# Attention stacks held in fixed halves of the rows, and a re-ordered opening, in a fused attention and convolution kernel

## The reference

```python
x = x + _L0_conv_ref(_gn(x), ...)   # 8-head attention over the 1024 pixels, head size 16
x = x + _L1_conv_ref(_gn(x), ...)   # 7x7 depthwise conv, layer norm over channels, MLP of 512, erf gelu
...
q = proj(Wq, bq, xh); k = proj(Wk, bk, xh); v = proj(Wv, bv, xh)
attn = jnp.einsum('bgdi,bgdj->bgij', q, k) * SCALE
attn = jax.nn.softmax(attn, axis=-1)
out = jnp.einsum('bgij,bgdj->bgdi', attn, v)
```

## Time and profile before

| | us |
|---|---|
| Median of 3 runs | 298.36 (298.24 to 299.01) |
| Profiled execution, its own time | 298.37 |
| Span of the profiled execution | 296.4 |
| PE busy | 287.5 (97%) |
| DVE busy | 233.8 (79%) |
| ACT busy | 181.1 (61%) |
| POOL busy | 79.4 (27%) |

### The profile page before, as it was taken

How to read it: one execution, slowest core, us unless ns; L and a number is a source line. 1 busy time by engine, 2 the same in 40 slices (tenths; PEclk the granted TensorE clock), 3 DMA queues, 4 the chain that set the end, 5 groups by cost and what they waited for, 6 DMA issues and landing times.

```text
span 296.4 us, 5468 instructions
## 1 busy us (share of the span) xinstructions
PE 287.5 (97%) x2104; PEld 116.9 (39%) x2106; DVE 233.8 (79%) x264; ACT 181.1 (61%) x354; POOL 79.4 (27%) x103
## 2 busy tenths in 40 slices
PE   7999999999999999999999999999999999999895
PEld 3544443343343443444343343344333444323342
DVE  2749889989989989988869989989995367986331
ACT  2342278878878878878878968875246644011421
POOL 7100633332000000000009788997020200101010
PEclk9999999999999999999999999999999999999999
DMA  7266003203303203303122387300000016720001
GB/s 241 50 121 102 11 0 58 50 8 54 54 3 56 51 9 56 54 3 54 18 40 48 110 169 170 81 1 3 1 2 0 2 26 156 186 83 0 0 35 35
DMA packets 8488, 16.30 MB, mean 55 GB/s; under 512 B 2564, under 2 KB 3716, under 8 KB 8464
## 3 DMA queue, kind: packets, MB, share of 16 engines
q1 hardware_dynamic: 8048, 15.29, 24.1%
q10 hardware_dynamic: 416, 0.69, 1.0%
HBM read 4.96 MB, written 1.73 MB: 23 GB/s over the span
## 4 chain that ended last, share of the span: by engine, by line
PE 90%; DVE 7%; POOL 1%; issue 1%; ACT 0%; DVEq 0%; POOLq 0%
PE ps L1054 25%; PE ps L1065 22%; PE ps L1153 10%; PE ps L1007 8%; PE ps L1211 5%; PE ps L1226 5%; DVE mx L770 4%; PE ps L979 4%; PE ps L945 3%; DVE ot L780 2%; PE ps L1044 1%; PE ps L956 1%; PE ps L1197 1%; PE ps L1169 1%; PE ps L1109 1%; PE ps L1246 1%
## 5 line engine op out<-in xcount | busy, mean ns | idle before, releaser
L770 DVE TENSOR_REDUCE mx<-ps 128x1 f32<-128x1024 f32 x128 | 155.5, 1223 | 20.2 <-PE ps L1007 19.2
L656 ACT ACTIVATE pr<-ps 128x512 f32<-128x512 f32 x256 | 139.3, 596 | 41.3 <-PE ps L1054 33.7
L1054 PE MATMUL ps<-qs,ks 50*128 50x512 f32 x256 | 98.1, 446 | 0.0
L1007 PE MATMUL ps<-ks,qs 48*128 48x512 f32 x256 | 94.5, 434 | 1.2 <-DVE mx L770 1.2
L1065 PE MATMUL ps<-pr,va 128*32 128x256 f32 x1024 | 81.5, 391 | 0.0
L1054 PEld LDWEIGHTS ps<-qs,ks 50*128 50x128 f32 x256 | 39.9, 185 | 56.0 <-ACT pr L656 40.4
L1007 PEld LDWEIGHTS ps<-ks,qs 48*128 48x128 f32 x256 | 39.7, 185 | 8.5 <-DVE mx L770 5.2
L1065 PEld LDWEIGHTS ps<-pr,va 128*32 128x32 f32 x1024 | 20.3, 108 | 44.2 <-ACT pr L656 24.8
L808 DVE SCALAR_TENSOR_TENSOR hl<-xpad,w,hl 128x512 f32<-128x512 f32 (+1 forms) x37 | 35.6, 962 | 0.9
L483 POOL CAST mparts<-mx 128x8 fp32r<-128x8 f32 x16 | 3.0, 190 | 121.4 <-DVE mx L770 121.4
L1153 PE MATMUL ps<-xr,wt 128*32 128x512 f32 x272 | 30.9, 593 | 0.0
(11 more groups left out here) (104 smaller groups left out, 201.2 us busy)
## 6 DMA issues: line engine op xcount, KB each, us to landing
qs<-hl SPq DMA_DIRECT2D x48, 64.0 KB, 2.4
ks<-hl SPq DMA_DIRECT2D x47, 64.0 KB, 2.4
xr<-xpad SPq DMA_DIRECT2D x16, 95.0 KB, 2.2
xr<-pad_dram SPq DMA_DIRECT2D x4, 361.0 KB, 6.5
xr<-pad_dram SPq DMA_DIRECT2D x4, 304.0 KB, 5.3
xr<-xpad SPq DMA_DIRECT2D x8, 76.0 KB, 2.1
xr<-xpad ACTq DMA_DIRECT2D x8, 76.0 KB, 2.2
xs<-x SPq DMA_DIRECT2D x2, 256.0 KB, 3.1
```

The costliest lines, as they stand in the source:

```text
L656: nc.scalar.activation(pr[:, n % PR, c * HALF:(c + 1) * HALF], bank("half", n, c), ACT.Exp, scale=SCALE).then_inc(exp_done, 1)
L770: nc.vector.tensor_reduce(mx[:, s % 2, i:i + 1], sm[(NT * s + i) % 2], AX.X, ALU.max).then_inc(max_done, 1)
L1007: last = nc.tensor.matmul(sm[k % 2][:, c * HALF:(c + 1) * HALF], qs[rows, cell_of(s) + i * P:cell_of(s) + (i + 1) * P], ks[rows, cell_of(s ...
L1054: nc.tensor.matmul(bank("half", n, c), ks[rows, cell_of(t) + j * P:cell_of(t) + (j + 1) * P], qs[rows, cell_of(t) + c * HALF:cell_of(t) + ...
```

## The change

Every head's stack now lies in both halves. The upper rows 64 to 111 (`MAXIMA`) are filled from `hl` as before and feed only `scores`; two DMAs of 48 rows then copy them to rows 0 to 47 (`VALUES`), which with the maxima's rows 48 and 49 feed only `scores_t`. `cell_of(t)` is `t % 3`. The six DMAs of a head are issued for head t + 2 in place of t + 3. In the opening, keys are projected first, the first head's queries go out in left and right halves of 512 columns, and all projections of the second image stand between the opening tiles, values first. The fillers between the opening tiles are gone.

```diff
-GROUP_ROWS = 64
+MAXIMA, VALUES = 64, 0
...
-    return (t // 4 * 2 + t % 2) % CELLS * N
+    return t % CELLS * N
...
-            return (bank("turn", s - 1) if s else mi)[0:PARTS * NT, 0:P]
+            return (bank("turn", s - 1) if s else st[0])[0:PARTS * NT, 0:P]
...
-        def stack(queue, i, t, n, blocks=range(TERMS)):
+        def stack(queue, i, t, n, blocks=range(TERMS), c=None):
 
             order, dst = ((Q_ORDER, qs), (K_ORDER, ks))[i]
-            queue.wait_ge(S(f"part{i}{n}", t // HEADS), 2 - t // HEADS)
+            queue.wait_ge(S(f"part{i}{n}", t // HEADS), 2 - t // HEADS if c is None else c + 1)
             h = t % HEADS
+            lo, hi = (0, N) if c is None else (c * HALF, (c + 1) * HALF)
             for g in blocks:
                 if order[g] == n:
                     queue.dma_start(
-                        dst[rows_of(t) + g * D:rows_of(t) + (g + 1) * D, cell_of(t):cell_of(t) + N].bitcast(F32),
-                        hl[h * D:(h + 1) * D, t // HEADS, i, n, :].bitcast(F32)).then_inc(S("stack", t), 16)
+                        dst[MAXIMA + g * D:MAXIMA + (g + 1) * D, cell_of(t) + lo:cell_of(t) + hi].bitcast(F32),
+                        hl[h * D:(h + 1) * D, t // HEADS, i, n, lo:hi].bitcast(F32))\
+                        .then_inc(S("stack", t) if c != 1 else S("stack_right"), 16)
+
+        def whole_stack(queue, t):
+
+            for n in range(PARTS):
+                for i in range(2):
+                    stack(queue, i, t, n)
+
+        def second_stack(queue, t):
+
+            queue.wait_ge(S("stack", t), 16 * 2 * TERMS)
+            if t == 0:
+                queue.wait_ge(S("stack_right"), 16 * TERMS)
+            cols = slice(cell_of(t), cell_of(t) + N)
+            for side in (qs, ks):
+                queue.dma_start(side[VALUES:VALUES + STACK, cols].bitcast(F32),
+                                side[MAXIMA:MAXIMA + STACK, cols].bitcast(F32)).then_inc(S("second", t), 16)
 
         inner = xpad[:, 0:PADDED].rearrange("p (a c) -> p a c", c=WIDE)[:, PAD:PAD + SIDE, PAD:PAD + SIDE]
 
@@ -392,37 +405,34 @@
             sp.dma_start(bv[:, :], bvrow.rearrange("a p -> p a")).then_inc(S("bv"), 16)
             sp.dma_start(w1s[:, :], w1).then_inc(S("w1"), 16)
...
+            for n in range(PARTS):
+                stack(sp, 1, 0, n)
+            stack(sp, 0, 0, 1, c=0)
+            for n in range(PARTS):
+                stack(sp, 0, 0, n, c=1)
+            whole_stack(sp, 1)
+            second_stack(sp, 0)
...
+            def next_stacks(t):
+
+                if t + 2 < T:
+                    sp.wait_ge(s_ready, NT * t)
+                    whole_stack(sp, t + 2)
+                if t >= 2:
+                    sp.wait_ge(st_ready, 2 * NT * (t - 1))
+                second_stack(sp, t + 1)
...
+                    if i == 0 and c == 0:
+                        stack(nc.scalar, 0, 0, 0, c=0)
             values(0)
+            values(1)
...
+            parts(1)
             copy_max(0)
-            values(1)
+            parts(0)
...
+            low_part(1, 0)
+            low_part(1, 1)
             low_part(0, 0)
             gn_spread(v, 1)
             low_part(0, 1)
-            low_part(1, 0)
             gn_vareps(v, 1)
-            low_part(1, 1)
...
                 if b:
-                    t_.wait_ge(*((S("va", 0), 1) if i else (S("bout"), 1)))
+                    t_.wait_ge(S("va", 1 - i), 1)
...
                 if b:
-                    t_.wait_ge(S("copied1"), 1)
+                    t_.wait_ge(S("xn", 1), 1)
+                    t_.wait_ge(S("bout"), 1)
+                    t_.wait_ge(S("b1"), 1)
...
+            project(0, 1)
+            gn_pe_mean(t_, 1)
             project(0, 0)
-            gn_pe_mean(t_, 1)
-            project(0, 1)
+            project_v(0, 0, NT)
             gn_pe_var(t_, 1)
-            project_v(0, 0, NT)
             first_bias()
             value_bias()
-            t_.wait_ge(S("b1"), 1)
-            project(1, 0)
...
+                if n == 1 and c == 0:
+                    t_.wait_ge(S("copied0"), 1)
                 if j == 0 and c == 0:
+                    t_.wait_ge(S("second", t), 32)
                     t_.wait_ge(s_mrow[t % 2], 16 * (t // 2 + 1))
-                rows = slice(rows_of(t), rows_of(t) + ROWS)
+                rows = slice(VALUES, VALUES + ROWS)
...
-                    if n < LATER:
+                    if 0 < n < LATER:
                         keep_busy(2)
...
-            keep_busy(3, sm[0][:, 0:HALF])
             for k in range(AHEAD):
+                if k == NT // 2:
+                    t_.wait_ge(S("stack_right"), 16 * TERMS)
                 for c in range(2):
                     scores(k, c)
                 if k in (1, 3):
-                    project(1, 1, k // 2, k // 2 + 1)
-                if k == 2:
-                    keep_busy(1, st[1])
-                if k == 4:
-                    t_.wait_ge(S("copied0"), 1)
-                if k in (7, 9):
-                    project_v(1, 2 * (k - 7), 2 * (k - 5))
+                    project_v(1, 2 * (k - 1), 2 * (k + 1))
+                if k in (5, 7):
+                    project(1, 1, (k - 5) // 2, (k - 3) // 2)
                 if k == 9:
+                    t_.wait_ge(S("copied1"), 1)
                     turn_max(0)
-                if k >= 4 and k not in (7, 9):
-                    keep_busy(2)
-            t_.wait_ge(S("kones"), 32)
-            t_.wait_ge(S("va", 1), 1)
+                if k in (9, 11):
+                    project(1, 0, (k - 9) // 2, (k - 7) // 2)
+            t_.wait_ge(S("kones"), 16)
+            t_.wait_ge(mt_done, 1)
```

More of the change, by code:

```diff
@@ L110, in uses_of_banks @@
     return uses
-def rows_of(t):
-    return t // 2 % 2 * GROUP_ROWS
 def cell_of(t):
-    return (t // 4 * 2 + t % 2) % CELLS * N
-def last_in_cell(t):
-    return max(s for s in range(t) if rows_of(s) == rows_of(t) and cell_of(s) == cell_of(t))
+    return t % CELLS * N
 def build(nc, x, wpack, bvrow, ones3, w1, w2, out):
@@ L402, in _ @@
             sp.wait_ge(S("minus"), 1)
[L403 to L411 removed]
+            sp.dma_start(
+                ks[VALUES + STACK:VALUES + ROWS, :].bitcast(F32).rearrange("p (a n) -> p a n", n=N),
+                minus[:, :].rearrange("p (a n) -> p a n", a=1).broadcast_to([PARTS, CELLS, N])).then_inc(S("kones"), 16)
@@ L494, in _ @@
             split_max(0)
-            for i in range(2):
+            for i in (1, 0):
                 low_part(i)
@@ L630, in _, with parts @@
                         .then_inc(S(f"part{i}0", 0), 1)
-            stack(nc.scalar, 1, 0, 0, (0,))
+                    if i == 0 and c == 0:
+                        stack(nc.scalar, 0, 0, 0, c=0)
             values(0)
-            for i in range(2):
+            values(1)
+            def parts(i):
                 a.wait_ge(S(f"proj{i}", 1), 2)
@@ L963, in value_bias @@
                 t_.wait_ge(S("w"), 16)
-                t_.wait_ge(S("gn_ve"), B)
-                nc.tensor.matmul(mi[:, GN_AT + 4 * B:GN_AT + 4 * B + 1], vec(C_WP, P), bv[:, :], start=True, stop=True)\
+                nc.tensor.matmul(bias_out, vec(C_WP, P), bv[:, :], start=True, stop=True)\
                     .then_inc(S("value_bias"), 1)
@@ L1005, in scores @@
                         t_.wait_ge(S("stack", s), 16 * 2 * TERMS)
-                rows = slice(rows_of(s), rows_of(s) + STACK)
+                rows = slice(MAXIMA, MAXIMA + STACK)
                 last = nc.tensor.matmul(sm[k % 2][:, c * HALF:(c + 1) * HALF],
```

40 lines of the change are left out of this document (12 added, 28 removed).

## The result

| | before | after |
|---|---|---|
| All executions | 298.24, 298.36, 299.01, 303.43 | 288.22, 290.63, 300.56, 323.8 |
| Median of these | 298.69 | 295.6 |
| Ratio of undisturbed runs | 1 | 0.9695 (0.9594 to 0.9796) |
| Profiled execution, its own time | 298.37 | 288.22 |
| Span of the profiled execution | 296.4 | 286.4 |

Mean granted clocks of the four executions after: 0.994, 0.982, 0.937 and 0.852, in the order of their times. So there are two results: at (nearly) full clock the kernel is some 10 us faster, where 11.8 was forecast; and it no longer holds that clock.

What follows compares the result with a forecast made beforehand. PE, busy 97% of the span, was taken to bound the kernel. From 298.37 us, - 9.6 (even heads) - 2.8 (opening) + 0.3 (fill) + 0.3 (GpSimd) gave 286.6 us, range 284.6 to 290.5 at 0.8.

Steps and rivals of the forecast that it cites:

- seven even heads: Heads 2, 4 to 14: with fixed halves all tiles pair, 1.37 us off each, 9.6 us in all.
- opening, until head 1: Opening: earlier first stack and maxima, paired tiles and fewer fillers, less new waits on ACT, save 2.8 us (1.5 to 3.8).
- fill behind head 12: Start of head 13: the small DMA row_max(13) waits behind the bulk fill, costing 0.3 us (0 to 1.5).
- GpSimd and DVE: Heads 12 and 13: a later GpSimd keeps DVE, and through it PE, longer, 0.3 us in all (0 to 1.5).
- clock: Granted clock over the kernel: the forecast sum held no loss for a fall, 0 us.
- the gap before the turn: Opening, before the first turn of the maxima: PE waits 0.9 us for ACT's second copy of the keys.
- the stepping: Opening: tile-by-tile reckoning of the 13 maxima after the first, DVE about 1.2 us each; first scores_t at 33.5.
- the reckoning of the stacks' lead: Fast heads: a stack issued for head t + 2 lands 1.1 us before scores needs it in tile 3; no cost.
- the rival: Opening without fillers: the clock falls, its 13 us of matmuls take twice that, 8 us more, 294.6 us; chance 0.04.
- The sign that the prediction named for itself: Before the first scores_t: a granted clock below 1.00 would show the prediction wrong.

Runs made afterwards that it cites:

- fill spread: The changed kernel with the fill's eight DMAs issued as 2, 3 and 3 in heads 12, 13 and 14; 300.29 to 311.98 us, none at full clock.
- the halves with all the fillers of before: The kernel before with fixed halves, second copy and lead of t + 2, its old opening kept; 288.74 and 289.98 us at full clock, 293.04 and 293.23 below.
- opening only: The changed kernel with the stacks of before and no second copy; 295.56 us at full clock, 309.04 to 312.39 below.
- turn in bank 7: The changed kernel with the first turn of the maxima in bank 7 in place of 4; none at full clock: 288.76, and 299.87 to 309.72 us.
- the four of six: The changed kernel with spread fill, fillers ahead of first scores, one behind every second opening tile, four before the turn; 286.58, 286.71 at full clock, 292.57 to 296.59 below.
- the one of six: As the four of six, with the turn in bank 7, fewer fillers there, head 3's stack one head earlier; 285.51 to 286.31 us at full clock, 305.81 below.

## Why the prediction was right, and where it failed

The forecast of 286.6 us comes close for the kernel at full clock, 286.96 to 288.22, and the ratio puts it at some 289, inside the range of 284.6 to 290.5. It doesn't hold for the median of all four executions, 295.6, which lies above the range. That the clock held, or nearly, in two of the first four is in part luck: of nine later executions of the same kernel only two did, 286.96 and 289.8. By terms, in the profiled execution:

| term | predicted | measured |
|---|---|---|
| seven even heads | -9.6 | 11.76 - 10.38 = 1.38 in head 2; -9.6 with the seven |
| opening, until head 1 | -2.8 | 43.56 - 47.29 = -3.7, and +0.6 at once in head 1 |
| fill behind head 12 | +0.3 | +1.4 |
| GpSimd and DVE | +0.3 | +0.15 in head 12 |
| clock | 0 | +0.9 in head 13 (12.3 us for 11.4); up to 323.8 - 287.0 = 37 in others |

The measured column adds up to some -10.2, and the execution's own time went from 298.37 to 288.22. In small part the terms made up for each other: the opening gave 0.3 us more than forecast, net of head 1, and the fill and the clock took 2.0 more.

**Pairing.** Right, and shown by the two kernels that hold one part each. From head 2's start to head 12's it took 162.47 - 54.54 = 107.93 us, for 172.44 - 57.67 = 114.77 before: 6.84 less, in five even heads 1.37 each. DVE at 10.22 of 10.38 us did not fall behind in a row of fast heads, as chosen.

**Opening.** Every mark came within 0.1 us or sooner: first `scores` 16.85 (16.8 predicted), first maximum 17.59 (17.8), the gap before the turn 1.01 (0.9), first `scores_t` 32.30 (33.5), tile 3 37.20 (38.0). Four maxima took 4.62 us, as in the earlier trace rows, some 1.15 each, and the stepping took 1.2: over a dozen maxima that is half of the 1.2 us by which the first `scores_t` came early. The opening alone gave 2.8 us at full clock. What was missed is head 1's fourth tile, 49.14 - 47.31 = 1.83 us for 1.23: the reckoning of the stacks' lead, 1.1 us, was made for a fast head in the middle, and head 0 is where the opening gains, so its stacks have less lead. Issuing that stack sooner took the 0.6 away.

**Fill.** Mechanism right, term mis-sized: 0.3 chosen between 0 and 1.5, and it was 1.4, next to the upper bound. PE waited 1.39 us for `row_max(13)`, and spreading the DMAs took it away. In the Trainium skill ("DMA: Bandwidth & Descriptors", Queues, rings and completion order) the descriptors of one issuing engine are consumed in ring order on each DMA engine. The trace is in line with it: PE went on 6.1 us after the issue of a small DMA behind the fill. It does not tell this from a small DMA that only had to share full engines, since the DMA share was 1.04 from 169.20 to 175.30.

**GpSimd and DVE.** DVE's operation on `ot` took 1.71 us, where the earlier trace rows had 1.54. (There it ended at 168.48 + 1.54 = 170.02, 0.15 us behind GpSimd's, not with it.) Head 12 with the fill spread takes 11.4 us. Before it took 12.6 with 1.37 of unpaired tiles, so 0.15 is left of this term. What ties DVE's time to GpSimd's was not tested.

**Clock.** This is the step that failed, in two ways. The prediction wrote "Against it, the granted clock is 1.00 in every window that I read" and gave the rival 0.04. But each of those windows was read with the fillers in place. They could not speak against a fall that comes when the fillers are gone. Taking out the fillers alone from the kernel before made seven of seven fall. And the rival was placed in the opening only, while the fill's term counted the wait at head 13 as time and put its effect on the clock at nothing. The two traces of the changed kernel both fell at head 13, behind that wait, and the halves with all the fillers of before fell there too. The sign that the prediction named for itself, "if the granted clock is below 1.00 before the first `scores_t`", is not in the changed kernel's two traces, but it is in all three of its variants with the bare new opening: opening only, fill spread, and turn in bank 7.

Twelve of thirteen executions of the changed kernel were below 1.00 in one place or the other (the 1353 us one aside, and counting the first profiled one, which fell for 3.4 us). Only two of them have traces, so how many fell in the opening is not known.

The size was off as well: the 8 us reckoned that only the opening's 13 us of matmuls would run slow, but a fall lasted up to 58 us in the traces, with PE busy for nearly all of it, in the opening and in the paired tiles behind it. Of the pauses in the opening, that for the first stack (0.5 to 0.6 us) and that for `copied0` (0.56 and 0.57) are where falls were seen to begin, and in the kernel before without fillers two waits for DVE (0.71 and 0.40). The longest one, 1.01 us before the turn, was followed by none in its trace.

The Trainium skill ("TensorE: Matmul & The Clock Gate", HAM oscillation) gives a bound for the idle gaps to avoid. The traces here don't bear that out as a safe bound: the pauses ahead of the falls, 0.4 to 1.4 us each, all lie under it.

**What stays open.** Why a fall lasts 3 us in one execution and 58 in another. Why the same pause at `copied0` was followed by a fall in one profiled execution (0.57 us) and not in another (0.55), and whether the four of six and the one of six that fell in those two kernels differ by more than chance. Whether the chip matters, and why the kernel before itself fell in 5 of 45. Whether the changed kernel would hold its clock with the fillers back but the fill not spread: the halves with the fillers of before, which is the nearest kernel, fell in two of four.

## What to carry to other kernels

Before you take out work that nobody reads, ask what it does for the clock, and test the removal by itself. A row that shows 1.00 with that work in place says nothing about the kernel without it. Look at all executions where a change can itself be what slows some of them. Price a new wait of PE at more than its own length: in one execution the fall behind a wait of 1.43 us came with 10.6 us more than at full clock. When two operands with few rows share the array, keep them in different halves for the whole kernel: here one copy by DMA, hidden by a head of matmuls, bought 1.38 us in every second head. And when a head gets shorter, re-read the queue of what is due at its end: a bulk transfer that just ended in time before is late after.

## What the runs showed of the hardware

- With PE's clock at 0.50, a stretch of 26.8 us in which PE was busy for all of 26.8 did not bring it back, nor did 54.4 us with 54.2 busy. It did come back in the end in each trace.
- It fell behind pauses of 0.4 to 1.4 us, in the opening and at head 13. Ahead of one fall PE was busy 5.53 of 6.90 us. Four traces of four with a wait of 1.29 to 1.43 us at head 13 fell behind it.
- At the very start the shown clock can mislead: the kernel before shows full clock in its first slices too, but its first eleven filler matmuls took 4.78 us, 0.43 each, and five later ones 1.24, under 0.25 each. The falls told of here show in durations as well (eight matmuls in 2.07 us for 1.16).
- Two `scores` matmuls started side by side with the two `scores_t` ahead of them in the queue, the first pair 0.02 us apart.
- A DMA of 48 rows by 1024 (192 KB) mostly costs SP no more to issue than one of 16 (0.54 and 0.59 us in head 12, against 0.59), and lands in 3.2 to 3.8 us (medians), where those of 16 rows (64 KB) take 2.3 to 2.4.
